# Identity matmuls on TensorE before its first matmul and in two places of the setup of a fused attention and low-rank linear kernel

## The reference

```python
def reference(x, ctx, g_xattn, g_ffn, W, b, lora_down, lora_up, down_aux, up_aux):
    s = einsum('bsd,bvd->bsv', layernorm(x), ctx)
    x = x + tanh(g_xattn[0]) * einsum('bsv,bvd->bsd', softmax(s), ctx)
    L = up_aux @ (lora_up @ (lora_down @ down_aux))
    z = layernorm(x)
    return x + tanh(g_ffn[0]) * (einsum('bsi,oi->bso', z, W) + b + einsum('bsi,oi->bso', z, L))
```

## Time and profile before

| | us |
|---|---|
| median of 3 runs | 319.59 (319.36 to 319.92) |
| the profiled execution, its own time | 316.71 |
| its span, first to last instruction | 314.9 |
| TensorE busy with matmuls in the span | 299.9 |
| TensorE's first matmul starts | 4.31 |
| first matmul of tile 0 starts (L481) | 19.35 |

### The profile page before, as it was taken

How to read it: one execution, slowest core, us unless ns; L and a number is a source line. 1 busy time by engine, 2 the same in 40 slices (tenths; PEclk the granted TensorE clock), 3 DMA queues, 4 the chain that set the end, 5 groups by cost and what they waited for, 6 DMA issues and landing times.

```text
span 314.9 us, 6478 instructions
## 1 busy us (share of the span) xinstructions
PE 299.9 (95%) x2072; PEld 283.3 (90%) x2072; DVE 234.6 (75%) x745; ACT 187.0 (59%) x546; POOL 221.3 (70%) x271
## 2 busy tenths in 40 slices
PE   4788999999999999999999999999999999999991
PEld 0668999998999999999899999999899999999981
DVE  3685778797588877798497778788587778777864
ACT  1674665656476565666466566656476665656651
POOL 3136777777577778777577877778488777887752
PEclk9999999999999999999999999999999999999998
DMA  7947254455398655555199765555198955443112
GB/s 218 412 184 192 91 191 166 176 202 203 126 262 263 221 193 200 200 202 203 65 260 288 233 223 200 202 185 180 39 285 282 275 203 201 166 177 127 67 46 89
DMA packets 17755, 60.60 MB, mean 192 GB/s; under 512 B 2360, under 2 KB 2360, under 8 KB 17722
## 3 DMA queue, kind: packets, MB, share of 16 engines
q1 hardware_dynamic: 17074, 59.26, 55.8%
q10 hardware_dynamic: 648, 0.95, 0.9%
HBM read 35.84 MB, written 16.78 MB: 167 GB/s over the span
## 4 chain that ended last, share of the span: by engine, by line
PE 90%; DMA 3%; ACT 1%; DVE 1%; SPq 1%; POOL 1%; issue 1%; POOLq 0%; DVEq 0%; ACTq 0%
PE y_ps L481 64%; PE y_ps L509 9%; PE a_ps L504 9%; PE c_ps L471 3%; DMA w_rows<-in_w 2%; PE y_ps L489 2%; DMA stacks<-v_lo 1%; SPq L220 1%; PE a_ps L471 1%; PE y_ps L539 1%; PE y_ps L548 1%; DVE o_sb L654 0%; ACT w_cent L412 0%; DVE x L616 0%; POOL x_bias L292 0%
## 5 line engine op out<-in xcount | busy, mean ns | idle before, releaser
L481 PE MATMUL y_ps<-wc,xT 128*128 128x334 f32 (+1 forms) x1536 | 228.1, 302 | 0.0
L481 PEld LDWEIGHTS y_ps<-wc,xT 128*128 128x128 f32 x1536 | 214.3, 189 | 2.0
L292 POOL TENSOR_TENSOR x_bias<-x,bias_g 128x512 f32<-128x512 f32 x63 | 81.1, 1288 | 65.4 <-DVE x L616 65.4
L280 POOL TENSOR_TENSOR xT<-xt_raw,xT 128x512 fp32r<-128x512 f32 x64 | 83.3, 1301 | 9.5 <-ACT xT L357 9.5
L372 ACT ACTIVATE expd<-y_ps,neg_max,rs 128x77 f32<-128x77 f32 x64 | 26.6, 416 | 81.9 <-DVE neg_max L606 81.9
L386 ACT ACTIVATE squares<-x,x_nmean 128x512 f32<-128x512 f32 x64 | 46.4, 725 | 18.7 <-DVE x_nmean L624 18.7
L303 POOL TENSOR_TENSOR rs<-stat_eps,half_neg 128x2 f32<-128x2 f32 (+1 forms) x67 | 46.1, 688 | 5.2
L654 DVE SCALAR_TENSOR_TENSOR o_sb<-y_ps,rs,x_bias 128x512 f32<-128x512 f32 x64 | 48.0, 751 | 1.6 <-POOL rs L303 1.6
L509 PEld LDWEIGHTS y_ps<-stacks,pT 109*128 109x128 f32 (+1 forms) x256 | 39.8, 191 | 5.4
L637 DVE TENSOR_TENSOR pT<-y_ps,pT 13x128 fp32r<-13x128 f32 x64 | 18.6, 290 | 34.9 <-ACT pT L363 34.9
L616 DVE SCALAR_TENSOR_TENSOR x<-a_ps,x_sb 128x512 f32<-128x512 f32 x64 | 43.7, 683 | 1.2 <-PE a_ps L504 1.2
(11 more groups left out here) (64 smaller groups left out, 181.1 us busy)
## 6 DMA issues: line engine op xcount, KB each, us to landing
xt_raw<-in_xt SPq DMA_DIRECT2D x32, 512.0 KB, 6.0
x_sb<-in_x SPq DMA_DIRECT2D x32, 512.0 KB, 5.0
out<-o_sb SPq DMA_DIRECT2D x31, 512.0 KB, 3.3
stacks<-v_hi SPq DMA_DIRECT2D x8, 308.0 KB
stacks<-v_hi SPq DMA_DIRECT2D x8, 256.0 KB
stacks<-v_lo SPq DMA_DIRECT2D x8, 256.0 KB
w_rows<-in_w ACTq DMA_DIRECT2D x1, 512.0 KB, 4.7
w_rows<-in_w SPq DMA_DIRECT2D x1, 512.0 KB, 7.6
```

The costliest lines, as they stand in the source:

```text
L280: pool.tensor_tensor(xT[:, k % TRING, 1, :, :], xt_raw[:, k % XRING // UNIT, k % UNIT, :, :], xT[:, k % TRING, 0, :, :].bitcast(F32), ALU. ...
L292: pool.tensor_tensor(x1_bias[:, q, :], x1[:, j, :], bias_g[:, :], ALU.add).then_inc(x1b_ready, 1)
L481: mm = pe.matmul(y_half(k, h)[:, 0:n], xT[:, k % TRING, part, c, :], wc[:, c, w, h * H:h * H + n], start=(c == 0 and part == 0 and w == 0) ...
```

## The change

A helper `stay_busy(count)` issues `count` matmuls of `ident` by `ident` in plain float32, 128 rows by 128 columns, into the first 128 columns of `y_ps`' pair 0. Nothing reads that result, and tile 0's first matmul there starts a new sum. TensorE runs twelve of them as its first work, sixteen between the transposes of W's two halves, and four between the context's transposes and its product with W. The wait for `ident` moves from ahead of the transposes to the head of the stream.

```diff
--- before.py
+++ after.py
@@ -437,6 +437,13 @@
         @block.tensor
         def _(pe):
 
+            def stay_busy(count):
+
+                for _ in range(count):
+                    pe.matmul(y_ps[:, 0, 0, 0:P], ident[:, :], ident[:, :], start=True, stop=True)
+
+            pe.wait_ge(ident_ok, 4)
+            stay_busy(12)
             pe.wait_ge(ld_in, 16)
             pe.matmul(a_ps[0:LR, :], low_in_sb[:, 0:LR], low_in_sb[:, LR:LR + D], start=True, stop=True)\
                 .then_inc(low_mm, 1)
@@ -539,8 +546,8 @@
                         pe.matmul(w_bank(c)[:, o * P:(o + 1) * P], w_cent[:, o, c * P:(c + 1) * P], ident[:, :],
                                   is_transpose=True, start=(o == 0), stop=False, skip_group_check=True)
 
-            pe.wait_ge(ident_ok, 4)
             w_transposes(0)
+            stay_busy(16)
             w_transposes(1)
             pe.wait_ge(dn_ok, 1)
             pe.wait_ge(up_ok, 1)
@@ -548,6 +555,7 @@
                 pe.matmul(w_bank(c), dn_st[:, c * P:(c + 1) * P], up_st[:, :], start=False, stop=True,
                           skip_group_check=True).then_inc(w_tr, 1)
             prep(0, TURN)
+            stay_busy(4)
             prep(0, PRODUCT)
             all_tiles(step, prep)
```

## The result

| | before | after |
|---|---|---|
| median of 9 runs, us | 319.36 (317.43 to 319.92) | 316.36 (315.77 to 317.22) |
| ratio, 95% interval | | 0.9909 (0.9883 to 0.9935) |
| the profiled execution: time, span | 316.71, 314.9 | 317.22, 315.4 |
| first matmul of tile 0, in the profile | 19.35 | 19.77 |

The kernel is 3.0 us faster, three times the forecast and outside its range. Yet the profiled execution is 0.5 us *longer* than the one of before. A comparison of these two profiles alone would call the change a loss.

A forecast was written before the change was run, and what follows sets the result against it. TensorE, busy 299.9 of 314.9 us, was taken to bound the kernel, its setup slowed by a low clock. A 1.2 us gain, less 0.5 x 0.5 and 0.05, gave 0.9: 319.59 - 0.9 = 318.7 us, range 318.0 to 321.8.

The forecast's parts named there:

- The clock as the one lever: Setup: the change acts only by useless early TensorE work, so that 11.63 to 15.1 us may run at the upper level.
- The third rival: Transfers into `stacks`, or `xT`: the lead is used up there and the time does not move, 319.6 us; chance 0.07.
- The cost of the fills: An identity matmul costs 0.43 us at 1.2 GHz, 0.21 at 2.4; at the lower level twelve cost 5.12, sixteen 6.83, four 1.71.
- the prediction's formula: Between W's halves: the sixteen end at 10.25 + (r - 1.6) / 2 us plus any wait; gain nil at r = 7.5.
- r: Time at which TensorE's clock rises with the change: bounds 5.1 and, from a stretch without a rise, 5.6 us; 5.6 taken.
- the lower bound of 5.1: Head of the stream: 3.5 us of unbroken work before the clock rises, counted from a start at 1.6 us.
- rival 1: Setup: the rise comes late, between 6.5 and 8.4 us; at 8.3 `ct` is 0.45 us late, 320.0 us; chance 0.15.
- Rival 2: Setup: float32 matmuls don't raise the clock before the banks' matmuls; + 7.2 us, 326.8, or half way 321.8; chance 0.2.
- The clock in those stretches: Setup before the change: from matmul spacing, the clock stood at the lower level to about 15.1 us and rose there.
- The stream with the change: Setup: with a rise at 5.1 us, `ct` and what follows come 1.2 us earlier, the most the change can give.
- the forecast's own range: Whole kernel: 318.1 us (1.5 us gained, if the timed runs before had a later rise than the profile) to 319.3.
- The 0.9: Whole kernel: forecast gain in us, 1.2 - 0.5 x 0.5 = 0.95 less 0.05 for starts behind idle stretches.

The follow-up runs named there:

- experiments 1 and 2: The kernel before, unchanged, run and profiled again twice: 319.16 us (ratio 0.9985) the first time, 319.38 us the second.
- Experiment 9: The changed kernel with its three fills as float32 transposes of the identity (24, 32 and 8) instead of matmuls: 316.09 us, ratio 0.9900.
- experiment 3: The kernel before with only the twelve identity matmuls at the head, without the sixteen and the four: 318.84 us, ratio 0.9996.
- experiment 8: The kernel before with eight identity matmuls at the head and eight between W's halves, none ahead of the product: 315.52 us, ratio 0.9874.

## Why the prediction was wrong

**The clock as the one lever: right.** The fills make the second half's transposes and the banks run at the upper level, and in every trace the rest of the span is the same, to 0.2 us: 314.9 - 19.35 = 295.6 us from tile 0's first matmul to the end in the first profile of before, 317.2 - 21.53 = 295.7 in the second, 315.4 - 19.77 = 295.6 and 314.4 - 18.68 = 295.7 in two of the changed kernel, 314.1 - 18.46 = 295.6 with eight and eight. All of the difference in span is when tile 0 starts. The third rival (the lead lost at the transfers) is thereby out.

**The cost of the fills: nearly right, slightly low.** Halves start 0.21 us apart at the lower level. At the upper they are 0.11 apart (3.74 - 0.28 = 3.46 us for 31 steps), where 0.107 was taken. By the prediction's formula the sixteen end at 12.15 for a rise at 5.4, and the transposes behind them started at 12.66; at 7.7 it is 13.3 and 13.74. The 0.45 to 0.5 us is the term's error: the first start takes 0.37 instead of 0.21, L448 and L451 keep 0.95 to 1.0 us each at the upper level instead of 0.91, and the sixteen take 0.16 more.

**Where r lies: in the bounds, not at them.** The rise came at 7.7, 5.4 and 6.1 with the changed kernel and the one without the four, 6.5, 7.1 and 5.9 with the others that begin with twelve. 5.6 was near the early end. The 3.5 us of unbroken work, from which the lower bound of 5.1 came, were no measure: with transposes the rise came 2.7 us after the start, and in experiments 1 and 2 the same second half's transposes and banks, as unbroken and as long, gave none.

**Rivals 1 and 2.** The profiled execution of after looks like rival 1 (tile 0 0.4 us later than in the profile of before, where it had 0.45), but that is in part luck: with its rise at 7.7 the prediction's formula, balanced at 7.5, gives a loss of 0.1 us, and the rest is what the fills cost more than was thought. Rival 2 is out in all eight traces that begin with identity matmuls or transposes.

**The step that failed** is the one in "The clock in those stretches" and "The stream with the change" that took the rise of before to be at 15.1 us in the timed runs as well, and carried a difference against 316.71 over to the median of 319.59. So the most that the change can give was put at 1.2 us. The times of before gave the warning, 2.9 us between the profiled execution and the median, and the forecast's own range allowed a gain of 1.5 us for it. In two of three profiles the rise is at 21.1 and 21.3, and the product then ends 2.2 us later. Against that execution the forecast would have been 0.9 + 2.2 = 3.1 us, against a measured 3.0. That this fits so well is in part luck. The 0.9 was itself too good: 316.71 - 0.9 = 315.8 where the median is 316.4, of which 0.45 us is the fills' error above. Without that error the sum is 3.1 - 0.45 = 2.65 us, near the 2.6 that the spans show below; the other 0.4 us of the measured gain was in no sum.

**What remains.** The median span of before (29 executions) is 317.1 and of after (9) 314.5: 2.6 us of the 3.0. The other 0.4 lies around the span, where 12 of these 29 executions have 3.0 us or more instead of 1.8 to 2.1, and none of the changed kernel's; nothing here explains it. Nor is it settled why the rise of before falls at 15.1 in one execution and past 21 in others; filling the small hole ahead of the product did not bring it forward, and no run tried the shapes of the matmuls between (L441, L444 and the product fill the array only in part), which stay a possible cause.

**Transposes raise the clock too.** Experiment 9 raised it with float32 transposes alone, at 4.3 us, earlier than in the profile of any other kernel here (5.4 to 7.7 with matmuls at the head). The Trainium skill, TensorE: Matmul & The Clock Gate, section "Part 4: PE-mode transpose", says that the full clock doesn't engage for transposes; for these it does not hold, and the measurement decides.

## What to carry to other kernels

Where one profiled execution differs from the median of the timed runs by more than the effect in question, profile the kernel before several times, and find what moves, ahead of any sum. A fill for TensorE's clock has two jobs, to raise it and to hold it over the next hole; the first alone was worth nothing (318.84 against 319.33 us). Its length is a cost once it outlasts the hole: twelve and twelve gave 315.84 us where twelve and sixteen, beside it, gave 316.40.

## What was not expected of the hardware

The clock's rise moves by several microseconds between executions of one program: 15.1, 21.1 and 21.3 us in the kernel before, 5.4 and 7.7 in the changed one. It fell at 12.7 us, behind a hole of 2.4 us that had ended at 11.83, in one execution (experiment 3) and stayed up over a hole of 1.75 us in another (experiment 8). The profile page's line of granted clock reads full for a stretch at the start that the durations show at half; only after a fall, as in experiment 3, does it show the lower level in the setup.
